# Expert 0's second and third pair of indirect adds issued on GpSimd ahead of the last four row scatters

## What is computed

```python
pos = (jnp.cumsum(oh, axis=0) * oh).sum(-1) - 1      # place of a token within its expert
keep = pos < cap                                     # cap = 1280 rows for an expert
xe = xp[buf_tok].reshape(E, cap, DIM)
h = silu(einsum(xe, w1)) * einsum(xe, w3)
out = einsum(h, w2) * buf_w.reshape(E, cap, 1)
y = zeros((N + 1, DIM)).at[buf_tok].add(out.reshape(E * cap, DIM))[:N]
z = silu(xf @ sw1) * (xf @ sw3) @ sw2                # the shared expert, every token
...
x + s * silu(y + z)
```

## Time and profile before

| | us |
|---|---|
| median of 3 runs | 1086.96 |
| the 3 runs | 1084.85, 1086.96, 1091.03 |
| the profiled execution, its own time | 1084.01 |
| its span | 1082.2 |
| mean granted TensorE clock | 0.983 of full |
| TensorE matmul busy | 993.8 (92% of the span) |
| GpSimd busy | 720.8 (67%) |

### The profile page before, as it was taken

One profiled execution on the slowest core, in us unless ns is written; L12 is line 12 of the kernel. 1 busy time (PEld: TensorE's weight loads), 2 busy tenths in 40 slices (PEclk: granted clock), 3 DMA queues, 4 the chain that ended last, 5 costly groups with the idle time before them and its releaser, 6 DMA issues.

```text
span 1082.2 us, 29821 instructions
## 1 busy us (share of the span) xinstructions
PE 993.8 (92%) x8059; PEld 949.1 (88%) x8059; DVE 782.9 (72%) x2542; ACT 589.8 (54%) x1129; POOL 720.8 (67%) x560
## 2 busy tenths in 40 slices
PE   5678898988888899999999999999999999999984
PEld 4668887887877899999999999999999999999931
DVE  6677888887777676677667776776777777777774
ACT  4668888888886344444444444444444444444453
POOL 1067777777777775767888766666666766676640
PEclk8799999999999999999999999999999999999998
DMA  9943443334444887978898887789778888987699
GB/s 274 303 164 128 143 143 140 137 134 145 145 143 147 257 202 150 201 144 174 167 182 156 165 195 155 147 196 203 159 164 195 172 192 182 194 195 146 142 299 348
DMA packets 174867, 195.57 MB, mean 181 GB/s; under 512 B 19865, under 2 KB 166594, under 8 KB 174786
## 3 DMA queue, kind: packets, MB, share of 16 engines
q1 hardware_dynamic: 120848, 123.15, 38.8%
q0 software_dynamic: 53312, 71.50, 34.2%
q10 hardware_dynamic: 626, 0.01, 0.0%
HBM read 92.15 MB, written 106.09 MB: 183 GB/s over the span
## 4 chain that ended last, share of the span: by engine, by line
PE 66%; POOL 9%; issue 7%; DVE 5%; ACT 5%; DMA 4%; SPq 2%; DVEq 0%; POOLq 0%; ACTq 0%
PE h L922 13%; PE h L924 13%; PE h L923 13%; POOL slot_rows L794 8%; PE yb L942 7%; PE yb L940 7%; PE yb L941 6%; PE xt L906 6%; DMA y_sum<-y_more,y_idx 1%; DMA slot_rows<-rows 1%; ACT rows L1182 1%; DVE act L1507 1%; SPq L472 1%; DVE raw L1516 1%; DMA x_all<-L_attn_x 1%
## 5 line engine op out<-in xcount | busy, mean ns | idle before, releaser
L922 PE MATMUL h<-xh,w_hl 128*128 (+1 forms) x1392 | 410.0, 295 | 4.3 <-DVE xl L1501 3.0
L924 PE MATMUL h<-xl,w_hl 128*128 (+1 forms) x1392 | 394.4, 283 | 0.0
L923 PE MATMUL h<-xh,w_hl 128*128 (+1 forms) x1392 | 393.0, 282 | 0.0
L759 POOL DMA_INDIRECT y_sum<-x_all,dest_top x168 | 267.4, 1592 | 109.7 <-DVE x_all L1778 62.1
L794 POOL DMA_INDIRECT slot_rows<-rows,dest_idx x256 | 261.0, 1020 | 110.8 <-issue 69.5
L1255 ACT ACTIVATE acth<-act 128x512 fp32r<-128x512 f32 x174 | 109.7, 631 | 316.9 <-PE yb L942 294.1
L922 PEld LDWEIGHTS h<-xh,w_hl 128*128 128x128 f32 x1392 | 264.4, 190 | 6.9 <-issue 5.8
L923 PEld LDWEIGHTS h<-xh,w_hl 128*128 128x128 f32 x1392 | 264.8, 190 | 0.0
L924 PEld LDWEIGHTS h<-xl,w_hl 128*128 128x128 f32 x1392 | 264.4, 190 | 0.0
L1511 DVE TENSOR_TENSOR actl<-act,acth 128x512 fp32r<-128x512 f32 x174 | 120.4, 692 | 181.5 <-ACT acth L1255 181.3
L940 PE MATMUL yb<-w_hl,acth 128*128 128x256 f32 x696 | 196.7, 283 | 3.9 <-DVE y_more L1778 2.7
(11 more groups left out here) (236 smaller groups left out, 1443.1 us busy)
## 6 DMA issues: line engine op xcount, KB each, us to landing
rows<-slot_rows SPq DMA_DIRECT2D x127, 289.0 KB, 3.5
raw<-L_ffn_w SPq DMA_DIRECT2D x99, 256.0 KB, 2.7
slot_rows<-rows SPq DMA_DIRECT2D x48, 289.0 KB, 9.4
x_all<-L_attn_x SPq DMA_DIRECT2D x16, 512.0 KB, 6.7
out<-s_all SPq DMA_DIRECT2D x32, 256.0 KB, 5.2
y_sum<-yw SPq DMA_DIRECT2D x31, 256.0 KB
x_all<-L_attn_x SPq DMA_DIRECT2D x20, 256.0 KB
x_all<-slot_rows SPq DMA_DIRECT2D x15, 289.0 KB, 3.8
```

The costliest lines, as they stand in the source:

```text
L759: pool.indirect_dma_start(y_dram, bass.IndirectOffsetOnAxis(y_index(buf, t), 0), y_out[buf][:, t, :], None, bounds_check=token_bound, oob_ ...
L922: mm(out, high, xh[:, k, cols], start=(k == 0), stop=False)
L923: mm(out, low, xh[:, k, cols], start=False, stop=False)
L924: ins = mm(out, high, xl[:, k, cols], start=False, stop=(k == KD - 1))
```

## The change

Within group 15, ahead of tile 3, POOL now issues the adds of pairs 0, 1 and 2 instead of pair 0 alone. The two calls that stood behind the last scatter are gone. Nothing is added or left out: four indirect accumulating DMAs (two tiles each for pairs 1 and 2) trade places with four indirect scatters, together with the four waits on `y_ready` that precede the adds. The waits for the landing of the adds, the queue of SP and all other engines' programs are as they were.

```diff
@@ -780,7 +780,8 @@
                     elif t == 3:
                         pool.wait_ge(z_stored, 16 * (A_PAIRS - 1))
                         pool.wait_ge(last_z_stored, 16)
-                        add_early(0)
+                        for q in range(3):
+                            add_early(q)
                     for k in range(K):
                         if k == K // 2:
                             if t == 0:
@@ -815,8 +816,6 @@
                             pool.wait_ge(first_added, first_adds(e))
                 slots(pool, count, body)
 
-            add_early(1)
-            add_early(2)
             pool.wait_ge(fifth_added, 32)
             pool.wait_ge(early_added[0], 32 * 2)
             for q in range(3, 6):
```

## The result

Over 20 runs of each the median went from 1086.41 to 1089.64 us; the ratio after to before is 1.0027, with a 95% interval of 1.0018 to 1.0037. That is 2.9 us more (2.0 to 4.0), which is slower, and inside the 0.5% that I had called no change. The time forecast, 1087.8 us, lies 1.8 us under the measured one and the range, 1084 to 1092.5, holds it.

The account below looks back on a forecast made before the run. TensorE was taken to bound the kernel behind 400 us. The terms 0 + 1.8 + 0 gave +1.8 us: 1085.8 us from the profile, 1088.8 from the median, 1087.8 chosen between, range 1084 to 1092.5.

Parts of the forecast that it names:

- POOL's gain at 0: POOL loses its 6.42 us wait and gains 6.1 us at pair 3's adds, worth 0 because TensorE waits for no add.
- The swap's 7.50 us: On POOL, the last four scatters are each issued 7.50 us later, behind the four adds of pairs 1 and 2.
- the place of the new wait: TensorE waits at pair 12's transposes, in the middle of pair 11, for rows SP loads 3.7 us later: 1.8 us.
- The wait of 1.8 us: Pair 12's rows land at 413.0 us, TensorE wants them at 411.2; bounds 0 to 3.5 us.
- The term for the scatter's landing: POOL's last scatter, started at 406.03 us, lands 1.79 us later, at 407.8; the upper bound allows 0.7 us more.
- The term for the load: SP's load of pair 12's rows, asked at 407.9 us, takes 5.1 us; bounds 3.1 to 6.1.
- The sum of +1.8 us: Whole kernel: 0 for POOL's gain, 1.8 us for TensorE's wait at pair 12, 0 for later loads.
- rival B: The wait at pair 12 also lowers TensorE's clock, losing 1.7 us: 3.5 us in sum, at most 5.2; chance 28%.
- Rival A: Pair 12's load takes 3.1 to 3.6 us and TensorE waits 0 to 0.3 us; 1084.0 or 1087.0 us; chance 18%.
- Rival C: Scatters held up behind adds in POOL's DMA queue: TensorE waits 7.6 us, 9.3 with lost clock, 1096.3 us; chance 5%.
- Rival D: POOL's backlog holds something unseen, so up to 6.1 us come back: 1077.9 or 1080.9 us; chance 4%.
- Later loads at 0: SP's loads for pairs 13 to 15 slip too but stay hidden from TensorE: 0 us.

Follow-up runs that it names:

- none_ahead: The kernel before the change, with the adds of all three pairs, pair 0 too, behind the last scatter: ratio 0.9996 (0.9986 to 1.0006).
- two_ahead: The changed kernel with only pairs 0 and 1 added ahead of the last four scatters, pair 2 behind: ratio 1.0000 (0.9989 to 1.0012).
- late_only: The kernel before, with POOL also waiting for pair 7's buffer before the last four scatters, adds left in place: ratio 1.0036 (1.0023 to 1.0049).
- again: The changed kernel without an edit, run once more: ratio 1.0020 (1.0006 to 1.0033) over 12 runs; TensorE waited 1.39 us for pair 12's rows.
- look2: The changed kernel without an edit, its third profile: no wait for pair 12's rows, 0.3 us more than before from restart to restart.
- count_split: The kernel before, with the last part of VectorE's count of fifth pairs moved from behind pair 3 to behind pair 4: ratio 0.9985 (0.9975 to 0.9996).

## Why the prediction was right, and where not

**What bounds the kernel, and POOL's gain at 0: right.** TensorE is the bound, and the early adds released nobody; `none_ahead` and `two_ahead` show it from both sides.

**The swap's 7.50 us and the place of the new wait: right**, to the pair and the engine. `late_only` shows the cause by itself, since it makes the scatters late and nothing early.

**The wait of 1.8 us: right by luck, by two errors that cancel.** The term for the scatter's landing, 1.79 us from one row 50 us earlier, measured 3.77 (2.6 to 4.5 over the profiles); the 0.7 us that the bounds allowed on it were too few in every profile that shows it. The term for the load, 5.1 us, measured 2.99 (3.0 to 4.4): I had taken it as slowed by pair 3's adds, and it ran faster than the quickest of the 17, 3.1 us. 1.79 + 5.1 = 6.9, and 3.77 + 2.99 = 6.8.

**The sum of +1.8 us: too small by over a third of the measured 2.9 us**, whose interval begins at 2.0. (By `again` alone, 2.2 us with 0.6 to 3.6, the 1.8 would be inside.) The weak step is the reading of one execution's margin as the margin: TensorE and POOL drift against each other by some us from one execution to the next, and in part of the executions rival B holds. I had given B 28%; in four profiles it was one, with 4.5 us at the wait and 2.9 us on the whole. So forecast and rival B were not two cases of which one would come true but two ends of one spread. That this spread makes up the missing 1.1 us is not shown: the four profiles cost 1.7 us in the mean, close to the forecast. (The upper end of the range, 1092.5, is not quite B's own 1092.2.)

**Rival A** (the load still in time) is the other end: look2. **Rival C** (scatters held up by the adds, over 5.4 us) did not come; the landing stayed at 4.5 us or less. **Rival D** had no case.

**Later loads at 0: right.** No wait of TensorE for rows of pair 13 to 15 shows in any profile, not even where pair 12's took 6.3 us.

## What to carry to other kernels

Work that is moved ahead in an in-order queue is paid by what it is moved past: look up who waits for the last item behind it, and how much margin that reader has, before counting what the moved work releases. Where two engines run at their own pace up to a meeting point, one trace's margin is a sample; take a second profile if the margin is smaller than the drift. And a margin that hides a delay today is used up when another gap is closed: the change cost 2.9 us on the kernel before and 5.7 us on the one without the count's gap.

## What the runs showed of the hardware

Between 376 and 430 us TensorE's granted clock went to the 1.2 GHz level behind single idle times of 2.0, 2.8 and 3.1 us, at a loss of 1.7 us of full clock each, and in nine profiles of ten behind one of 2.2 us, for the same 1.7 us. Behind 3.74, 4.3 and 6.3 us the loss was 3.4 us (for the last 0.90 + 1.0 + 1.0 + 0.52 by the four stretches above, a part of it while TensorE was still waiting). It stayed up behind 1.39, 1.46, 1.60 and 1.71 us.

This is no rule of the gap's length, and the expectation of `look2`, which says that every gap of 2.0 us and more was followed by a fall, was wrong when it was written. The tenth profile had the same 2.22 us gap and no fall. At about 350 us TensorE waits in every profile for the first rows of the second phase, for 1.5 to 2.2 us, and in 13 profiles of 14 the clock stayed at 1.00 from 340 to 376 us; here the longest of these waits, in `none_ahead`, and the clock around it. And the 2.70 us wait near 1035 us, with one of 1.33 us behind it, was followed by a loss of 1.7 us in 4 profiles, of 3.4 us in 8 and of nothing in 2, `count_split` and `again`, whose stretch is the last line:

```profile
350.83 0.66 PE L905 MATMUL xt<-ident,x_all 128*128 128x128 f32 x4 [2.23 <-DMA x_all<-slot_rows]
```

```profile
340.00:376.00 36.00, 30.27 (x253) 1.00 0.76 227
```

```profile
1030.00:1050.00 20.00, 15.32 (x45) 1.00 0.99 288
```

So an idle time of 2 to 3 us has more than one price, and one trace shows one of them. Shortening such a gap can bring more than its own length: `count_split` took hardly any waiting away and still brought 0.15%.

The standing of two engines to each other, POOL's last scatter against TensorE's restart, varied by 4.5 us over four profiles at one kernel, while the times of its 20 runs lie within 3.5 us to either side of their median. Where a profile has the same events on TensorE the time repeats much more closely: 652.20, 652.21 and 652.17 us from restart to restart in `before`, `two_ahead` and `none_ahead`.
